# Three score banks, and the unscaling of a row maximum moved behind the low plane, in an attention stage of a one-core kernel

## The reference

```python
x = L0_attn_x                                    # 16 x 256 x 128: 4096 rows
x = x + 0.5 * ffn(layernorm(x))                  # 8 experts, argmax gate, 128 -> 512 -> 128
x = x + attn(layernorm(x), context)              # 8 heads of 128, 512 keys
x = x + 0.5 * ffn(layernorm(x))

# attn, per head
sim = q @ k.T * SCALE
sim = (sim - mean(sim)) * 1.5 + mean(sim)
out = softmax(sim) @ v                           # heads concatenated, then @ Wout + bout
```

## Time and profile before

| | |
|---|---|
| median of three runs | 742.47 us |
| the profiled execution | 742.75 us, its span 740.9 us |
| maxima of the attention units | first starts at 142.5 us, last at 623.0 us |
| busy TensorE, VectorE, ScalarE, GpSimd | 94%, 88%, 71%, 50% of the span |
| granted TensorE clock, mean | 0.988 |

### The profile page before, as it was taken

One profiled execution on the slowest core, in us unless ns is written; L12 is line 12 of the kernel. 1 busy time (PEld: TensorE's weight loads), 2 busy tenths in 40 slices (PEclk: granted clock), 3 DMA queues, 4 the chain that ended last, 5 costly groups with the idle time before them and its releaser, 6 DMA issues.

```text
span 740.9 us, 15537 instructions
## 1 busy us (share of the span) xinstructions
PE 693.1 (94%) x4376; PEld 471.2 (64%) x4376; DVE 654.9 (88%) x1910; ACT 523.2 (71%) x1219; POOL 374.1 (50%) x507
## 2 busy tenths in 40 slices
PE   8988999989999999999999999999999998989992
PEld 7767888755556555655655656555565554769991
DVE  6989999998898999899899989899989988788881
ACT  4786777678778678778767867867876776546661
POOL 5067888344344345346336435534634633586662
PEclk9999999999999999999999999999999999999995
DMA  9941433210000000000000000000000011232210
GB/s 249 345 147 37 83 78 82 56 45 0 1 1 1 1 5 12 1 2 14 1 1 12 5 1 7 10 0 5 12 1 1 16 45 66 92 92 67 52 47 5
DMA packets 31795, 31.51 MB, mean 43 GB/s; under 512 B 5050, under 2 KB 26184, under 8 KB 31201
## 3 DMA queue, kind: packets, MB, share of 16 engines
q1 hardware_dynamic: 27360, 23.91, 11.2%
q0 software_dynamic: 3520, 6.40, 3.4%
q10 hardware_dynamic: 832, 0.21, 0.1%
HBM read 20.96 MB, written 10.47 MB: 42 GB/s over the span
## 4 chain that ended last, share of the span: by engine, by line
PE 52%; DVE 36%; issue 5%; POOL 2%; ACT 1%; DMA 1%; DVEq 1%; another core or an unknown queue 0%; POOLq 0%; SPq 0%; ACTq 0%
PE bank L1551 10%; PE bank L1553 10%; PE bank L1552 10%; DVE neg_max L1433 10%; DVE probsT_lo L1442 9%; PE bank L1772 8%; PE bank L1600 5%; DVE neg_max_unscaled L1436 3%; PE bank L1586 3%; DVE hT_lo L1287 2%; PE bank L1603 2%; DMA rows<-in_L_attn_x 1%; POOL rows L616 1%; DVE h L1266 1%; PE bank L1610 1%
## 5 line engine op out<-in xcount | busy, mean ns | idle before, releaser
L632 POOL TENSOR_SCALAR probs<-probs,row_inv 128x512 f32<-128x512 f32 x256 | 178.3, 697 | 266.6 <-DVE row_inv L1447 255.3
L858 ACT ACTIVATE probs<-bank,neg_max_unscaled,unscale_bits 128x512 f32<-128x512 f32 x256 | 199.2, 778 | 115.7 <-DVE neg_max_unscaled L1436 113.2
L1433 DVE TENSOR_REDUCE neg_max<-bank 128x1 f32<-128x512 f32 x256 | 176.0, 687 | 23.9 <-PE bank L1553 18.4
L1442 DVE TENSOR_TENSOR probsT_lo<-bank,probsT_hi 128x512 f16<-128x512 f32 x256 | 174.5, 682 | 1.7 <-ACT probsT_hi L867 1.7
L1772 PEld LDWEIGHTS bank<-ident,probs 128*128 128x128 f32 x1024 | 125.6, 141 | 66.0 <-issue 18.0
L1772 PE MATMUL bank<-ident,probs 128*128 128x128 f32 x1024 | 154.7, 274 | 9.1 <-DVE probsT_lo L1442 7.5
L867 ACT ACTIVATE probsT_hi<-bank 128x512 f16<-128x512 f32 x256 | 150.3, 587 | 1.7 <-PE bank L1772 1.7
L1551 PE MATMUL bank<-probsT_hi,vw_hi 128*128 128x512 f16 x256 | 97.6, 381 | 7.6 <-DVE probsT_lo L1442 6.8
L1551 PE MATMUL bank<-m_hi,xT_hi 128*128 128x512 f16 x256 | 97.0, 379 | 0.0
L1552 PE MATMUL bank<-probsT_lo,vw_hi 128*128 128x512 f16 x256 | 97.0, 379 | 0.0
L1553 PE MATMUL bank<-probsT_hi,vw_lo 128*128 128x512 f16 x256 | 97.0, 379 | 0.0
(11 more groups left out here) (239 smaller groups left out, 1197.1 us busy)
## 6 DMA issues: line engine op xcount, KB each, us to landing
b<-in_L_ffn_b SPq DMA_DIRECT2D x4, 1024.0 KB, 9.2
x_packed<-slot_rows SPq DMA_DIRECT2D x39, 65.5 KB
slot_rows<-slots SPq DMA_DIRECT2D x39, 65.5 KB, 1.8
x_stats<-rows SPq DMA_DIRECT2D x4, 524.0 KB, 10.3
rows<-x_packed SPq DMA_DIRECT2D x8, 262.0 KB, 2.6
rows<-in_L_attn_x SPq DMA_DIRECT2D x4, 512.0 KB, 8.3
w_lo<-in_L_ffn_w SPq DMA_DIRECT2D x8, 256.0 KB, 6.7
w_hi_lo<-in_L_ffn_w SPq DMA_DIRECT2D x8, 256.0 KB, 13.0
```

What stands on the lines that cost most here:

```text
L632: pool.tensor_scalar(PR[:, u % 4, :], PR[:, u % 4, :], RI[:, u % 4:u % 4 + 1], 2.0 ** P_BITS, ALU.mult, ALU.mult).then_inc(normed, 1)
L858: act.activation(PR[:, n % 4, :], BK[n % 2][:, :], ACT.Exp, bias=NMS[:, n % 4:n % 4 + 1], scale=MUN, accum_out=SU[:, n % 4:n % 4 + 1]).the ...
L1433: v.tensor_reduce(NM[:, n % 4:n % 4 + 1], BK[n % 2][:, :], AX.X, ALU.max, negate=True)\
L1442: v.tensor_tensor(PTL[at], BK[2 + u % 2][:, :].rearrange("p (c q) -> p c q", c=KC), PTH[at], ALU.subtract).then_inc(pT_lo, 1)
```

## The change

- A function `score_bank(u)` gives the bank of a unit's scores: still `u % 2` for the first four units (FIRST_UNITS = 4), then banks 6, 0, 1 in turn. From unit 4 on, scores wait for the exp of unit u - 3 in place of u - 2. At unit 4 TensorE also waits until the first expert pass has read its last outputs out of banks 6 and 7.
- The transposed rows of the next group no longer go to bank 6 but to `4 + job % 2` (`turn_bank`), a bank of the value sums, with a wait for the group that used it last (`o_kept`).
- On VectorE the unscaling of the maximum (one 128 x 1 instruction per unit) moves from directly behind the maximum to behind the low plane of unit n - 4.

```diff
+        def score_bank(u):
+
+            return BK[u % 2] if u < FIRST_UNITS else BK[(6, 0, 1)[(u - FIRST_UNITS) % 3]]
+
+        def turn_bank(job):
+
+            return 4 + job % 2 if job else 1
...
+        FIRST_UNITS = SLOTS + 5 - SCORES_AT
...
-                    act.activation(PR[:, n % 4, :], BK[n % 2][:, :], ACT.Exp, bias=NMS[:, n % 4:n % 4 + 1],
+                    act.activation(PR[:, n % 4, :], score_bank(n)[:, :], ACT.Exp, bias=NMS[:, n % 4:n % 4 + 1],
...
-                    ln_keep(g, 6)
+                    ln_keep(g, turn_bank(g))
...
                 if unit(n):
                     dve.wait_ge(scores, n + 1)
-                    v.tensor_reduce(NM[:, n % 4:n % 4 + 1], BK[n % 2][:, :], AX.X, ALU.max, negate=True)\
+                    v.tensor_reduce(NM[:, n % 4:n % 4 + 1], score_bank(n)[:, :], AX.X, ALU.max, negate=True)\
                         .then_inc(neg_max, 1)
-                    dve.wait_ge(neg_max, n + 1)
-                    v.tensor_scalar(NMS[:, n % 4:n % 4 + 1], NM[:, n % 4:n % 4 + 1], MUN, None, ALU.mult)\
-                        .then_inc(neg_max_ready, 1)
                 if unit(n - LAG_T - 1):
                     u = n - LAG_T - 1
                     dve.wait_ge(pT_hi, u + 1)
                     at = (slice(None), (u // G) % 2, slice(None), slice((u % G) * P, (u % G + 1) * P))
                     v.tensor_tensor(PTL[at], BK[2 + u % 2][:, :].rearrange("p (c q) -> p c q", c=KC),
                                     PTH[at], ALU.subtract).then_inc(pT_lo, 1)
+                if unit(n):
+                    dve.wait_ge(neg_max, n + 1)
+                    v.tensor_scalar(NMS[:, n % 4:n % 4 + 1], NM[:, n % 4:n % 4 + 1], MUN, None, ALU.mult)\
+                        .then_inc(neg_max_ready, 1)
...
-                        xT_low(g, 6, slice(half * 2 * P, (half + 1) * 2 * P))
+                        xT_low(g, turn_bank(g), slice(half * 2 * P, (half + 1) * 2 * P))
...
+                    if u == FIRST_UNITS:
+                        pe.wait_ge(s_yhi, SLOTS)
+                        pe.wait_ge(s_ylo, SLOTS)
                     if u >= 2:
-                        pe.wait_ge(probs, u - 1)
+                        pe.wait_ge(probs, u - 1 if u < FIRST_UNITS else u - 2)
                     cols = slice(i * P, (i + 1) * P)
-                    three(BK[u % 2][:, :], AXH[:, g % 2, cols], AXL[:, g % 2, cols], MH[:, h, :], ML[:, h, :],
+                    three(score_bank(u)[:, :], AXH[:, g % 2, cols], AXL[:, g % 2, cols], MH[:, h, :], ML[:, h, :],
...
                     pe.wait_ge(xT_lo, g)
-                    xn_transposes(g, 6)
+                    if g >= 2:
+                        pe.wait_ge(o_kept, g - 1)
+                    xn_transposes(g, turn_bank(g))
```

More of the change, by code:

```diff
@@ L836, in step @@
                         act.wait_ge(s_hb, LOW_TILES)
-                        ln_keep(0, 1)
+                        ln_keep(0, turn_bank(0))
                     if r == 0 and m > SCORES_AT:
@@ L1321, in step @@
                         dve.wait_ge(s_hb, LOW_TILES)
-                        xT_low(0, 1, slice(0, G * P))
+                        xT_low(0, turn_bank(0), slice(0, G * P))
                     if r == 0 and m >= SCORES_AT:
@@ L1626, in step @@
                         pe.wait_ge(xn_first, 1)
-                        xn_transposes(0, 1)
+                        xn_transposes(0, turn_bank(0))
                     if r == 0 and m >= SCORES_AT:
```

## The result

| | before | changed |
|---|---|---|
| median | 742.57 us (4 runs) | 832.15 us (4 runs) |
| range | 740.56 to 746.61 | 830.14 to 832.84 |
| ratio, with its 95% interval | | 1.120 [1.116, 1.124] |
| span of the profiled execution | 740.9 us | 831.0 us |

The account below looks back on a forecast made before the run. TensorE, 1.73 us per unit, was taken to bound most slots; the change would make a loop the bound. Stage 564.8 + 2.6 + 0.5 = 567.9 for 472.8 us, +95 on 742.75: 838 us, range 825 to 850.

Parts of the forecast that it names:

- The loop: Attention stage: unscaling, exp, high plane, low plane, next unscaling form a closed loop; 2.25 us per unit, 564.8 us; chance 0.87.
- The side steps: VectorE's and ScalarE's extra steps in attention slots: mostly covered by waiting; 2.6 us for seven groups on VectorE, nothing on ScalarE.
- the first turn: At unit 4 the unscaling moves from 0.73 to 1.22 us behind the maximum: 0.5 us.
- Outside the stage: After the last unscaling of the attention stage the order of waits is the same: 0.
- The third bank: TensorE may write scores one exp earlier, but is not late in the loop: worth 0.
- the waits at unit 4 and for `o_kept`: TensorE's waits for expert outputs to be read and for an evacuation 11 slots back: 0.
- VectorE's saving: The unscaling no longer waits for the maximum's end: about 0.1 us per slot, 25 us of VectorE time, worth nothing.
- The clock: TensorE 77% busy in the stage keeps its granted clock: 0. Rival, clock swings: 858 to 958 us, chance 0.04.
- the rule that I held against this change: Small idle times between matmuls cycling through PSUM banks can make TensorE's clock swing: 858 to 958 us, chance 0.04.
- The faster one: Rival: the loop does not bind, bank and VectorE saving win TensorE's idle 13 us: 730 us, chance 0.03.
- The signs: Unscalings 2.25 us apart, low planes waiting some 200 us in all, exp waiting about 0.9, stage end near 719 us.

Follow-up runs that it names:

- e2: Kernel before, two score banks, with only the unscaling moved behind the low plane: 828.6 us, ratio 1.118 to the kernel before.
- e3: Changed kernel with ScalarE's high plane of unit n - 3 put ahead of the exp of unit n: 727.1 us, ratio 0.983 to the kernel before.
- e4: Changed kernel with the reciprocal of unit n - 1 put ahead of the unscaling of unit n: 843.7 us, ratio 1.141 to the kernel before.
- e1: Changed kernel with the unscaling put back directly behind the maximum, three score banks kept: 740.0 us, ratio 1.001 to the kernel before.
- e5: Kernel before, two score banks, with only ScalarE's high plane put ahead of the exp: 739.4 us, ratio 1.000 to the kernel before.
- e6: Changed kernel, three score banks, with the unscaling back behind the maximum and ScalarE's high plane ahead of the exp: 739.9 us, ratio 1.000.
- e8: Changed kernel with high plane ahead of the exp and VectorE's order maximum, reciprocal, unscaling, low plane: 729.6 us, ratio 0.986 to the kernel before.
- e7: Kernel before, two score banks, with unscaling behind the low plane and high plane ahead of the exp: 729.8 us, ratio 0.986.

## Why the prediction was right, by its steps

**The loop.** Right, and the whole of the result. It was found from the order of two lists and priced from a trace in which it cost nothing: there one turn spanned two slots. The four legs were taken at 0.25, 0.77, 0.63 and 0.61 and came out at 0.24, 0.77, 0.62 and 0.61. Taken at 2.25, it is 2.237 in the mean of the 237 slots without a long side step: 251 x 0.013, some 3.3 us too much. e2 shows that the move alone makes it, e3 that it is this loop (cut, it is gone), e4 that each 0.06 us on it is paid 251 times.

**The side steps.** Covered, as said, but I put 2.6 us on them. In the changed kernel the longest one stands like this:

```profile
383.74 0.36 DVE L1230 BATCH_NORM_AGGREGATE mean_var<-bn 128x2 f32<-128x6 f32 x4
...
384.04 0.70 POOL L642 TENSOR_SCALAR probs<-probs,row_inv 128x512 f32<-128x512 f32 x1 [0.34 <-DVE row_inv L1458]
384.14 0.63 DVE L1233 TENSOR_SCALAR var_eps<-mean_var 128x4 f32<-128x4 f32 x1
...
384.67 0.68 DVE L1443 TENSOR_REDUCE neg_max<-bank 128x1 f32<-128x512 f32 x1
```

0.93 us where the earlier trace rows had 1.15, and the slot is 2.31 us, 0.07 over the loop's; two side steps of each group reach that, the 14 distances above, 0.9 us in all and 1.7 less than I put. The instance of rows 8 was not an odd one: in the kernel before five of seven groups have it at 1.14 or 1.15. The step itself is shorter in the changed kernel, for `var_eps` takes 0.61 to 0.63 us there in all seven groups, and 0.84 in those five. Beside it runs GpSimd's scaling of the probabilities, at 384.04 above, and in the kernel before:

```profile
281.72 0.84 DVE L1223 TENSOR_SCALAR var_eps<-mean_var 128x4 f32<-128x4 f32 x1
281.82 0.70 POOL L632 TENSOR_SCALAR probs<-probs,row_inv 128x512 f32<-128x512 f32 x1
```

Both times `var_eps` ends 0.03 or 0.04 us behind the scaling. The length that I took over from the kernel before thus went with how two engines meet there, and the change moved that. The stage was forecast at 567.4 from unit 4 on (without the first turn) and is 562.4: 3.3 us of the loop and 1.7 of the side steps.

**Outside the stage.** Forecast 0; measured +1.5 ahead of it besides the first turn, -1.4 behind it. Both are within the spread of executions: over the ten traces unit 4's unscaling comes at 150.9 to 154.2 us and the part behind unit 255's takes 111.3 to 117.2, while the stage is 472.1 to 472.8 us in all four kernels with the unscaling directly behind the maximum. The rest of 838 against 832.15 is the profiled execution, 832.84, itself 0.7 over the median.

**The third bank and the waits at unit 4 and for `o_kept`: 0.** Right in this kernel: e1 and e2.

**VectorE's saving: 25 us, worth nothing here.** Right in the changed kernel, and it was there to be had: with the loop cut, the slot is 1.38 in place of 1.52 and the kernel 12 us faster (e3 beside e1, e5 and e6). The saving per slot was 0.14, where I took 0.1: what stood 0.71 behind the maximum now stands 0.60 behind it (385.27, behind the maximum at 384.67 above), and the rest is hundredths at the other steps. What I had not seen is how many slots it would reach: I wrote that in most slots the chain runs through TensorE alone, but in the kernel before only 91 of the 251 distances of maxima are 1.73 us; in e3 it is 134.

**The clock.** It stayed at 1.00, its 2.4 GHz level, with TensorE 384.6 us busy in 450 (windows, 155 to 605 us), that is 85% as the profile counts, and 0.5 us of slack in a turn. So the rule that I held against this change, of banks cycled with small idle times (the Trainium skill, "TensorE: Matmul & The Clock Gate", section "A second HAM failure mode: psum-queue depth-cycling"), was not borne out in this kernel; the longest idle time of TensorE in the stage is 0.96 us.

**The rivals.** The faster one fell with e1 for the bank, and was bound to 730 us by TensorE's 13 us of idle time. That bound was wrong: e3 has a median of 727. From unit 4 to unit 255 it gains 11.4 us, but TensorE's recorded idle time fell only from 13.8 to 7.6. A 512-column matmul is recorded as 0.38 us while the next starts after 0.22, so a stall of up to 0.16 us behind it leaves no idle time in the record, and a longer one shows with 0.16 less. Counted by starts (what each distance to the next start has over the usual 0.22, or 0.11 for a transpose) TensorE lost 23.5 us before and 12.2 in e3, 11.3 less, which is the gain; the rest, its work, is 449 or 450 us in every kernel. So the bound should have been 742.75 - 23.5 = 719 us. In the changed kernel TensorE works 449 of 562 us, 80%, where the record says 86% and I forecast 77%; my 1.73 us per unit had left out the extra transposes of some slots.

**The signs.** Unscalings 2.24 apart (2.25 forecast), low planes that wait 0.77 us in slots without side steps (0.8), the end of the stage at 715.2 us (719): as said. Two were too large: all low planes wait 143 us in 233 places, where I wrote some 200 in nearly all of 252, since most slots have a side step that uses part of the wait; and the exp's wait is 0.88 us in a plain slot, 203.7 us in all 256.

## What to carry to other kernels

Before an instruction is moved behind a wait, follow what it releases all the way round: if another engine's in-order list leads back to that wait, the move turns a chain over two slots into one turn per slot, and buffers don't help. The waits of the old trace don't warn (1.7 us here), but start-to-start distances along the loop do: they gave a slowdown of 95 us where 90 was measured. And look for the partner of a good move: the same move lost 90 us and, with two instructions of ScalarE exchanged, gained 12. Before an experiment that gave the expected time is called a confirmation, read in its trace whether the time was saved where it was expected: in e8 it was not.

## What the runs showed of the hardware that was not expected

On VectorE an instruction that needs the result of the one ahead starts 0.70 to 0.73 us behind the start of a 128 x 512 maximum, an independent one 0.59 to 0.61. Of the 0.1 us only 0.03 is idle time in the record, and no list of waits shows it, as VectorE waits for its own instruction; filled with the low plane, it was worth 1.7% of the kernel (e3 beside e6).

The side step `var_eps` on VectorE (128 x 4) ended 0.02 to 0.03 us behind GpSimd's scaling of 128 x 512 probabilities wherever the two met. It took 0.17 us with no scaling beside it (e8, two groups), 0.48 to 0.50 where the scaling had begun 0.23 us earlier (e4), 0.61 where it had begun 0.11 earlier, 0.75 where it began 0.03 later (e5, e7) and 0.84 where it began 0.11 later (before). The record shows a long instruction and no wait. `logits` (L1404), with two inputs, took 0.40 us where the scaling had begun 0.3 earlier (e6) and 0.19 where it began 0.09 later (changed). That GpSimd holds such an instruction up is read from these times; no run was made for it.
